# The last two attention steps of a fused linear-attention and routed-expert kernel: slots before attention rows, routing and plan before queries, unpaced scatters, first loads that wait for less

## The chip, the core and the metric

The kernel runs on one core of a Trainium2 chip. The metric is the device time of one launch in microseconds (us). A core has five engines with a queue each, which meet only at semaphores: PE (TensorE, matmuls), DVE (VectorE), ACT (ScalarE), POOL (GpSimd) and SP (SyncE, which here only issues DMAs).

## The reference

Input `x` is 16 batches of 512 tokens of width 256. The output is `x` plus a linear attention of the normalised rows plus a mixture of experts of the same rows.

```python
xn = layernorm(x)
Q, K, V = elu(xn @ Wq.T + bq) + 1, elu(xn @ Wk.T + bk) + 1, xn @ Wv.T + bv
attn = (Q @ (K.T @ V)) / (Q . (K.sum over tokens + 1e-6)) @ Wo.T + bo
scores = sigmoid(xn @ gate.T)           # 16 experts in 4 groups
# the best 2 groups by their two best scores, then the best 4 experts,
# weights = scores / their sum * 2.5
moe = sum over the 4 experts of weight * (silu(xn @ up[e]) @ down[e])
shared = silu(xn @ shared_up) @ shared_down
out = x + attn + moe + shared
```

## The kernel before, in words

There are two phases. In the **first phase** a loop over `c` = 0 to 15 (`B` = 16) takes one batch of 512 tokens a step: normalise, turn on PE, keys, queries, the product of keys and rows (`m`), its product with the folded output weights (`p`), the attention rows (`c_done`, `attention_rows`), and the shared expert in four parts (`up`, `down`, ending in `shared_sum`, which sets `y_summed`). Each fp32 product is made as three fp32r matmuls of a high and a low half (`split3`, L319); the halves are split by ACT (a cast) and DVE (a subtraction, the `..._low` and `..._split` functions).

Routing goes alongside, on DVE: `route_scores` to `route_experts` choose four experts for each token, PE counts ranks (`rank_batch`), `route_slots` and `route_chain` turn the ranks into row numbers and set `route_ready`. POOL then writes each normalised row, with its weights, to its slot in a buffer in HBM sorted by expert (`rows_by_expert`): 16 indirect scatters of 128 rows a batch, 12 of half rows (`scatter_row`, L498) and 4 of whole rows (`scatter_first`, L504), the latter with the sum of `x`, attention and shared expert in the second half. In the loop each scatter waits for a point of PE's work (pacing); those of batch c run during step c + 1. The last step has no successor: batch 14 is scattered in it, and batch 15 after it.

After the last routing DVE makes the **plan** (`count_units`, `plan_units`, `plan_rows`): which 256 rows each of the 143 units (`UNITS`) takes, of which expert, and which scatters must have landed before. PE turns it (L1482, L1484), DVE writes it as `table` (L1252) and as packed expert numbers (`packed`, L1258, `plan_ready`), and the engines load both into registers.

In the **second phase** unit u takes 256 rows of one expert. SP loads the first halves of its rows (`load_rows`, L428, 7 units ahead) and the second halves (`load_sums`, L438, 4 ahead). PE turns the rows (`turn_rows`), does the up product, and the down product (`unit_down`, sets `fd_done`); ACT casts and applies silu; DVE weighs and adds (`sum_up`, L1291, sets `y_ready`); POOL scatters the sums onward to the token's next slot with two indirect DMAs of 128 half rows (L587, L590 for the last units). PE's order in iteration u is up(u), turn(u + 2), down(u - 1), so rows u + 2 that are late hold unit u - 1 as well. From unit 6 on POOL also waits until PE is a unit ahead (`fd_done` of u + 2). In iteration 12 SP first loads one expert's weights into the only raw buffer, which is free when DVE has made the halves of the one before (`set_low`, iteration 6).

Which loads wait for batch 15: `load_rows` of units below 8 (`EARLY`) for what the table says, `load_sums(4)` for all its scatters, because the buffers `f_y[4]` to `f_y[7]` lie where the rows of batch 15 are scattered from; `load_rows(4)` for its attention rows.

## Time and profile before

| | us |
|---|---|
| median of 3 runs | 843.58 (842.2 to 844.42) |
| the profiled execution's own time | 846.81 |
| its span, first to last instruction | 845.1 |
| first phase, to the end of batch 15's scatters on POOL | about 455 |
| second phase, from the first unit's scatter on POOL | 457.9 to 836 |

The page has, over the span, PE 88% busy, DVE 83%, POOL 69%, ACT 68%; the issue of a DMA is not counted as busy. The span is to be read in two parts, since the phases have different limits, and at the seam between them.

### The profile page before, as it was taken

How to read it: one execution, taken by the hardware profiler on the slowest of the kernel's cores; microseconds unless marked ns; L12 is line 12 of the kernel's file. 1: busy time of each engine (PE TensorE's matmuls, PEld its weight loads, DVE VectorE, ACT ScalarE, POOL GpSimd, SP SyncE). 2: the span in 40 equal slices, each digit the busy share in tenths (PEclk: the TensorE clock that was granted, in tenths of full speed). 3: DMA queues.
4: the chain of work that ended last, by engine and by line, in shares of the span. 5: the costliest groups of instructions: out<-in, count | busy, mean ns of one | idle time of the engine just before them, and what ended most of it. 6: DMA issues, size and time to landing. Idle time of an engine off the chain costs nothing.

```text
span 845.1 us, 19794 instructions
## 1 busy us (share of the span) xinstructions
PE 744.0 (88%) x5232; PEld 678.8 (80%) x5232; DVE 698.6 (83%) x2401; ACT 572.8 (68%) x1174; POOL 581.7 (69%) x581
## 2 busy tenths in 40 slices
PE   4999999999999999999968798888979897989671
PEld 3899999999999999999857787777778777878661
DVE  5989999999999999999996788778868787878661
ACT  4877778777778777787615687676757676767540
POOL 1056777777677777776776677777777777777753
PEclk9999999999999999999997999999999999999985
DMA  6245544556445544433338999999999999999988
GB/s 178 69 158 202 206 155 166 200 184 216 174 147 198 184 157 147 144 123 117 114 134 275 297 352 309 328 337 333 342 319 319 323 348 325 330 331 338 332 267 271
DMA packets 142317, 199.66 MB, mean 236 GB/s; under 512 B 16752, under 2 KB 117760, under 8 KB 142208
## 3 DMA queue, kind: packets, MB, share of 16 engines
q1 hardware_dynamic: 111152, 113.41, 43.0%
q0 software_dynamic: 28064, 81.93, 25.2%
q10 hardware_dynamic: 2992, 3.06, 1.2%
q8 instruction: 45, 0.74, 0.4%
q14 instruction: 64, 0.52, 0.2%
HBM read 104.19 MB, written 105.04 MB: 248 GB/s over the span
## 4 chain that ended last, share of the span: by engine, by line
PE 46%; DMA 17%; DVE 16%; issue 9%; POOL 6%; SPq 3%; ACT 1%; DVEq 1%; ACTq 0%; POOLq 0%
PE bank_a L319 21%; PE bank_x L319 10%; PE bank_y L319 9%; DMA xn<-rows_by_expert 8%; DMA rows_by_expert<-xn,f_id 7%; DVE xn L1291 3%; POOL rows_by_expert L587 3%; PE bank_a L1495 3%; DMA x_in<-rows_by_expert 3%; DVE hs_l L1304 2%; POOL rows_by_expert L498 2%; PE bank_a L1334 1%; SPq L326 1%; SPq L438 1%; DVE w L1270 1%
## 5 line engine op out<-in xcount | busy, mean ns | idle before, releaser
L587 POOL DMA_INDIRECT rows_by_expert<-xn,f_id x256 | 249.8, 976 | 85.6 <-issue 50.6
L498 POOL DMA_INDIRECT rows_by_expert<-xn,slots_now x192 | 197.2, 1027 | 103.1 <-issue 44.3
L721 ACT CAST xt_h<-bank_a 128x512 fp32r<-128x512 f32 x143 | 84.0, 587 | 68.2 <-PE bank_a L1495 63.2
L1273 DVE TENSOR_TENSOR xt_l<-bank_a,xt_h 128x512 fp32r<-128x512 f32 x143 | 98.1, 686 | 23.9 <-ACT xt_h L721 23.4
L319 PE MATMUL bank_y<-ws,hs_h 128*128 128x256 f32 x512 | 96.4, 286 | 0.5 <-DVE hs_l L1029 0.5
L504 POOL DMA_INDIRECT rows_by_expert<-xn,slots_now x64 | 80.7, 1260 | 17.9 <-issue 14.2
L319 PE MATMUL bank_x<-xt_h,ws 128*128 128x512 f32 x256 | 92.0, 400 | 0.1
L752 ACT ACTIVATE hid<-bank_x 128x256 f32<-128x256 f32 x143 | 55.0, 384 | 53.9 <-PE bank_x L319 44.7
L319 PEld LDWEIGHTS bank_y<-ws,hs_h 128*128 128x128 f32 x512 | 82.6, 192 | 4.0 <-DVE hs_l L1029 0.7
L319 PE MATMUL bank_y<-ws,hs_l 128*128 128x256 f32 x256 | 73.2, 286 | 0.0
L319 PE MATMUL bank_y<-we,hs_h 128*128 x284 | 63.5, 316 | 10.9 <-DVE hs_l L1304 7.1
L319 PE MATMUL bank_a<-we,hs_h 128*128 x288 | 64.0, 315 | 9.5 <-DVE hs_l L1304 5.7
L669 ACT ACTIVATE k_f<-bank_a,minus_one 128x256 f32<-128x256 f32 x64 | 30.4, 476 | 54.7 <-issue 27.0
L1495 PE MATMUL bank_a<-ident,xn 128*128 128x128 f32 x288 | 47.9, 291 | 21.7 <-DMA xn<-rows_by_expert 21.2
L319 PE MATMUL bank_x<-xt_h,k_h 128*128 128x256 f32 x288 | 65.6, 290 | 0.1
L319 PE MATMUL bank_x<-xt_h,k_l_p 128*128 128x256 f32 x284 | 64.5, 289 | 0.4 <-DVE xt_l L1273 0.4
L1291 DVE SCALAR_TENSOR_TENSOR xn<-bank_a,w,xn 128x256 f32<-128x256 f32 x144 | 62.6, 475 | 0.8 <-PE bank_a L319 0.8
L1495 PE MATMUL bank_a<-ident,x_in 128*128 128x128 f32 x284 | 45.5, 283 | 19.9 <-DMA x_in<-rows_by_expert 19.1
L319 PEld LDWEIGHTS bank_y<-we,hs_h 128*128 128x128 f32 x284 | 46.1, 196 | 20.2 <-issue 18.7
L1291 DVE SCALAR_TENSOR_TENSOR xn<-bank_y,w,xn 128x256 f32<-128x256 f32 x142 | 61.7, 475 | 0.0
L1304 DVE TENSOR_TENSOR hs_l<-hid,hs_h 128x256 fp32r<-128x256 f32 x143 | 59.6, 417 | 2.5 <-ACT hs_h L757 2.5
L319 PEld LDWEIGHTS bank_a<-we,hs_h 128*128 128x128 f32 x288 | 46.3, 194 | 18.3 <-issue 17.5
(287 smaller groups left out, 2429.6 us busy)
## 6 DMA issues: line engine op xcount, KB each, us to landing
xn<-rows_by_expert SPq DMA_DIRECT2D x204, 272.0 KB, 4.8
x_in<-rows_by_expert SPq DMA_DIRECT2D x71, 272.0 KB
rows_by_expert<-spare SPq DMA_DIRECT2D x22, 544.0 KB, 5.4
x_in<-in_L_attn_x_dram SPq DMA_DIRECT2D x16, 512.0 KB, 4.0
out_dram<-rows_by_expert SPq DMA_DIRECT2D x8, 1024.0 KB, 14.9
rows_by_expert<-xn,f_id POOLq DMA_INDIRECT x286
rows_by_expert<-xn,slots_now POOLq DMA_INDIRECT x256
xn<-rows_by_expert ACTq DMA_DIRECT2D x11, 272.0 KB, 6.6
```

The lines of the kernel that those rows point to most:

```text
L319: last = nc.tensor.matmul(dst, a, b, start=start and k == 0, stop=stop and k == n - 1, skip_group_check=mixed)
L326: fours[engine, i] = fours.get((engine, i), ())[-4:] + nc.values_load_multi_w_load_instructions(table[i:i + 1, u // P, u % P:u % P + 4], e ...
L498: G.indirect_dma_start(out=half_rows[:, :], in_=xn[:, c % NB, s, 0:RW], in_offset=None, out_offset=bass.IndirectOffsetOnAxis(ap=slots_now[ ...
L504: G.indirect_dma_start(out=by_expert[:, :], in_=xn[:, c % NB, s, :], in_offset=None, out_offset=bass.IndirectOffsetOnAxis(ap=slots_now[:, ...
L587: G.indirect_dma_start(out=half_rows[:, :], in_=f_y[u % YB][:, tile], in_offset=None, out_offset=offset).then_inc(added[u % CLS], 16)
L669: S_.activation(k_f[:, s, :], A[s][:, 0:D], ACT.Exp, bias=minus_one[:, 0:1])
L721: S_.copy(f_h[u % 4], A[u % 2][:, :].rearrange("p (c s t) -> p c s t", c=KD, s=2)).then_inc(fx_hi, 1)
L752: S_.activation(f_hid[u % 2], X[u % 2][:, 0:UR], ACT.Silu).then_inc(fs_done, 1)
L1273: V.tensor_tensor(f_l[u % 4], A[u % 2][:, :].rearrange("p (c s t) -> p c s t", c=KD, s=2), f_h[u % 4].bitcast(F32), ALU.subtract).then_inc ...
L1291: last = V.scalar_tensor_tensor(out=y, in0=f_dn[u % 2][tile][:, 0:D], scalar=w2[:, u % 4, tile:tile + 1], in1=y, op0=ALU.mult, op1=ALU.add)
L1304: V.tensor_tensor(f_hl[u % 2], f_hid[u % 2], f_hh[u % 2].bitcast(F32), ALU.subtract).then_inc(fh_lo, 1)
L1495: last = T_.transpose(A[u % 2][:, (2 * h + tile) * P:(2 * h + tile + 1) * P], f_rows[u % RB][:, tile, h * P:(h + 1) * P], ident[:, :])
```

## The change

Five groups of edits, all around the last two steps (c = 14 and c = 15) and the first units:

1. **Step 14**: PE counts the ranks before the attention rows and DVE does `route_slots` and `route_chain` before `attention_rows`. One shared `down` moves from behind the keys of step 15 to ahead of them. The keys of step 15 go to the banks in the order in which the attention rows free them (`key_bank`), the ranks to another bank (`rank_bank`).
2. **Step 15 and the plan**: on DVE the routing of batch 15 comes right after the keys, and the whole plan before the `queries`, the low halves of queries and products, and the attention rows. PE puts the ranks before `m`, and the attention rows behind the turned plan. The table and the packed numbers are signalled apart (`table_ready`), and SP waits only for the table. Each of PE, DVE and ACT loads one word of expert numbers (six units) at first and the other 23 in iteration 2.
3. **POOL**: the scatters of batches 13, 14 and 15 wait for `route_ready` and `y_summed` only, in the order 12 half-row scatters, 4 whole-row scatters. The wait for PE's lead starts at unit 10, not 6.
4. **SP's first loads**: `f_y[4]` to `f_y[7]` move to other memory. The sums of units 4 to 6 are loaded before the rows of unit 7 and no longer wait for batch 15's scatters; the rows of unit 8 do (as they did, by their place in the queue).
5. **Expert weights**: one more expert's weights are made in the second phase. Loads stand in SP's iterations 12 and 26 (12 alone before), the splitting in iterations 3 to 6, 16 to 20 and 30 to 34. In iteration 1 PE does `unit_down(0)` before `turn_rows(2)`.

```diff
--- before.py
+++ after.py
...
-        per_batch = reused(q_f, (2, B + 1, E))
-        table = reused(q_f, (2, P), 0, COLS).bitcast(U32)
...
+        per_batch = reused(k_f, (2, B + 1, E), E * E + 8 * E)
+        table = reused(k_f, (2, P), 0, COLS).bitcast(U32)
...
-        f_y = [reused(xn, (2, RW), (i + 4) % 8 * 2 * RW) for i in range(YB)]
+        f_y = [reused(xn, (2, RW), (i + 4) * 2 * RW) for i in range(4)]
+        f_y += [reused(k_f, (2, RW), SUB * D - 2 * RW), reused(q_f, (2, RW)), reused(spare, (2, RW)),
+                reused(x_in, (2, RW), 4 * 2 * RW)]
...
-        LAST_SET_LOADED = 12
+        SET_LOADED = {12: SH + E - 2, 26: SH + E - 1}
+        SET_SHAPED = {3: SH + E - 3, 16: SH + E - 2, 30: SH + E - 1}
+        SET_HIGH = {4: SH + E - 3, 18: SH + E - 2, 32: SH + E - 1}
+        SET_LOW = {6: SH + E - 3, 20: SH + E - 2, 34: SH + E - 1}
...
+        def key_bank(c, s):
+            return A[(s + 2) % SUB if c == B - 1 else s]
+
+        def rank_bank(c):
+            return X[0 if c >= B - 2 else 1]
...
-                load_set(c + 3)
+                if c + 1 < B:
+                    load_set(c + 3)
...
-            sp.wait_ge(plan_ready, 1)
+            sp.wait_ge(table_ready, 1)
...
+                if u == EARLY:
+                    sp.wait_ge(scattered[(B - 1) % NB], scatters_until(B - 1))
                 sp.dma_start(f_rows[u % RB], unit_rows(row, 0)).then_inc(rows_loaded[u % RB], 16)
 
             def load_sums(u):
-                if u == 4:
-                    sp.wait_ge(scattered[(B - 1) % NB], scatters_until(B - 1))
+                if u == 5:
+                    sp.wait_ge(q_lo, B)
                 if u >= YB:
                     sp.wait_ge(added[(u - YB) % CLS], adds_until(u - YB))
                 for k in range(CLS):
...
+                if u in SET_LOADED:
+                    load_set(SET_LOADED[u])
+                if u == EARLY - 1:
+                    for v in range(EARLY // 2, EARLY - 1):
+                        load_sums(v)
                 if u < UNITS:
                     load_rows(u)
-                if 0 <= u - (ROWS_AHEAD - SUMS_AHEAD) < SUMS_BY_ACT:
-                    load_sums(u - (ROWS_AHEAD - SUMS_AHEAD))
+                v = u - (ROWS_AHEAD - SUMS_AHEAD)
+                if 0 <= v < EARLY // 2 or EARLY - 1 <= v < SUMS_BY_ACT:
+                    load_sums(v)
...
-            for c in range(B):
+            for c in range(B - 2):
...
+            ROWS = SUB * (TOP_K - 1)
+            scatter_row(B - 4, 10)
+            scatter_row(B - 4, 11)
+            pool.wait_ge(attn_ready, SUB * (B - 2))
...
+            for c in range(B - 3, B):
+                pool.wait_ge(route_ready, c + 1)
+                for n in range(ROWS):
+                    if c == B - 3 and n == 7:
+                        inverse_root(B - 1)
+                    scatter_row(c, n)
+                pool.wait_ge(y_summed, c + 1)
+                for s in range(SUB):
+                    scatter_first(c, s)
 
...
-                    if u >= 6:
+                    if u >= 10:
...
+            def queries_high(c):
+                act.wait_ge(q_ready, KD * (c + 1))
+                wait(act, c_done, SUB * c)
+                S_.copy(q_h[:, :, :], q_f[:, :, :]).then_inc(q_hi, 1)
...
+            queries_high(B - 1)
...
-                if c >= 1:
+                if 1 <= c < B - 1:
                     route_chain(c - 1)
                 for s in range(SUB):
                     dve.wait_ge(k_exp, SUB * c + s + 1)
...
                 route_scores()
+                if not after:
+                    route_inverse(c)
+                    route_group_scores()
+                    route_groups()
+                    route_top()
+                    route_experts()
+                    rows_split(c)
+                    dve.wait_ge(k_hi, c + 1)
+                    dve.wait_ge(c_done, SUB * c)
+                    V.tensor_tensor(k_l[:, :, :], k_f[:, :, :], k_h[:, :, :].bitcast(F32), ALU.subtract
+                                    ).then_inc(k_lo, 1)
+                    route_slots(c)
+                    shared_sum(c - 1)
+                    route_weights(c)
+                    route_chain(c)
+                    dve.wait_ge(m_hi, c + 1)
+                    V.tensor_tensor(m_l[:, :, :], A[2][:, :].rearrange("p (c d) -> p c d", c=KD),
+                                    m_h[:, :, :].bitcast(F32), ALU.subtract).then_inc(m_lo, 1)
+                    hidden_low(n)
+                    hidden_low(n + 1)
+                    count_units()
+                    plan_units()
+                    break
...
+                if c == B - 2:
+                    route_slots(c)
+                    route_chain(c)
+                    attention_rows(c)
+                    hidden_low(n + 3)
+                    continue
...
+            queries(B - 1)
             hidden_low(SH * B - 2)
-            hidden_low(SH * B - 1)
             dve.wait_ge(plan_turned, 1)
+            V.tensor_copy(table, X[0][0:COLS, 0:UR].rearrange("p (j u) -> p j u", j=2)).then_inc(table_ready, 1)
+            products_low(B - 1)
+            dve.wait_ge(plan_turned, 2)
...
             V.tensor_copy(packed, packed_f).then_inc(plan_ready, 1)
+            queries_split(B - 1)
+            hidden_low(SH * B - 1)
             attention_rows(B - 1)
             dve.wait_ge(attn_ready, SUB * B)
             shared_sum(B - 1)
 
             dve.wait_ge(plan_ready, 1)
-            experts = load_experts(mybir.EngineType.DVE)
+            experts = load_experts(mybir.EngineType.DVE, slice(0, 1))
...
                 for s in range(SUB):
-                    if s < 2:
+                    if not after:
+                        pe.wait_ge(attn_ready, SUB * (c - 1) + s + 1)
+                    elif s < 2:
                         wait(pe, attn_ready, SUB * (c - 1) + s + 3)
...
+                elif after:
                     down(n - 2)
                 for h in range(KD):
-                    pe.wait_ge(k_ready, SUB * c + h + 1)
+                    pe.wait_ge(k_ready, SUB * c + h + (1 if after else 3))
...
+                if not after:
+                    pe.wait_ge(silu_done, n + 1)
+                    rank_batch(c, rank_bank(c))
...
-                else:
-                    pe.wait_ge(q_ready, KD * (c + 1))
-                    rank_batch(c, A[0])
...
-                if after:
-                    up(n + 3, par)
+                if not after:
+                    break
+                up(n + 3, par)
+                if c == B - 2:
+                    pe.wait_ge(silu_done, n + 3)
+                    rank_batch(c, rank_bank(c))
                 pe.wait_ge(p_lo, KD * (c + 1))
                 pe.wait_ge(q_lo, c + 1)
                 for s in range(SUB):
-                    if s >= 2 and after:
+                    if s >= 2:
                         pe.wait_ge(xt_lo, KD * (c + 1) + s - 1)
-                    if s == 2 and not after:
-                        pe.wait_ge(rank_read, c + 1)
+                    attend(c, s)
+                if c == B - 2:
+                    down(n + 2)
+                    pe.wait_ge(rank_read, c + 1)
+                else:
                     pe.wait_ge(silu_done, n + SH)
-                    rank_batch(c, X[1])
-                if after:
-                    up(n + SH, (c + 1) % 2)
-                else:
-                    for i in range(2):
-                        down(n + i)
-                        up(n + 2 + i, par)
-
+                    rank_batch(c, rank_bank(c))
+                up(n + SH, (c + 1) % 2)
+
+            down(SH * B - 4)
+            down(SH * B - 3)
+            pe.wait_ge(rank_read, B)
+            up(SH * B - 2, (B - 1) % 2)
+            up(SH * B - 1, (B - 1) % 2)
             pe.wait_ge(plan_made, 1)
             pe.wait_ge(silu_done, SH * B)
...
+                last.then_inc(plan_turned, 1)
             down(SH * B - 2)
+            pe.wait_ge(p_lo, KD * B)
+            pe.wait_ge(q_lo, B)
+            for s in range(SUB):
+                attend(B - 1, s)
             down(SH * B - 1)
...
                 if u == 1:
+                    unit_down(0)
                     turn_rows(2)
-                    unit_down(0)
+                    unit_down(1)
                     turn_rows(3)
-                    unit_down(1)
...
```

Where instructions stand now and then, first on DVE from the end of the plan (the writes of `u_tab`) to the shared sum of batch 15. Before:

```order
L1167 TENSOR_SCALAR u_tab<-u_class_n 128x4x2
L1029 TENSOR_TENSOR hs_l<-hid,hs_h 128x512 x2
L1252 CAST q_f<-bank_x 7x256
L1253 TENSOR_TENSOR q_f<-bank_x,place 1x144
L1256 TENSOR_REDUCE q_f<-q_f 1x24
L1258 CAST q_f<-q_f 1x24
L1058 RECIPROCAL rz<-bank_a 128x2
L1061 SCALAR_TENSOR_TENSOR xn<-bank_a,rz,x_in 128x256 x2
L1058 RECIPROCAL rz<-bank_a 128x2
L1061 SCALAR_TENSOR_TENSOR xn<-bank_a,rz,x_in 128x256 x2
L1045 TENSOR_TENSOR xn<-bank_y,xn 128x4x256
```

After (L1067 queries, L1056 hidden low half, L1293 table, L1084 products' low halves, L1296 to L1301 packed numbers, L1072 queries' low half, L1091 first of the attention rows):

```order
L1200 TENSOR_SCALAR u_tab<-u_class_n 128x4x2
L1067 SCALAR_TENSOR_TENSOR q_f<-q_f,bank_a 128x512 x2
L1056 TENSOR_TENSOR hs_l<-hid,hs_h 128x512
L1293 CAST k_f<-bank_x 7x256
L1084 TENSOR_TENSOR k_l_p<-bank_a,k_l_p 128x258 x2
L1296 TENSOR_TENSOR k_f<-bank_x,place 1x144
L1299 TENSOR_REDUCE k_f<-k_f 1x24
L1301 CAST k_f<-k_f 1x24
L1072 TENSOR_TENSOR q_l<-q_f,q_h 128x1024
L1056 TENSOR_TENSOR hs_l<-hid,hs_h 128x512
L1091 RECIPROCAL rz<-bank_a 128x2
```

The queries' two instructions and the low halves of queries and products now stand behind the plan; they stood before it.

On POOL, towards the end of the first phase. Before (`x12` counts DMAs in a row; the first row is the last 6 half-row scatters of batch 13 and the first 6 of batch 14, the 18 are the last 6 of batch 14 and the 12 of batch 15):

```order
L498 DMA rows_by_expert<-xn,slots_now 237568x272 x12
L534 MEMSET x_in 128x256
L536 AFFINE_SELECT x_in<-x_in 128x256
L504 DMA rows_by_expert<-xn,slots_now 118784x544 x4
L498 DMA rows_by_expert<-xn,slots_now 237568x272 x18
L504 DMA rows_by_expert<-xn,slots_now 118784x544 x4
```

After, from the first half row of batch 13 on:

```order
L520 DMA rows_by_expert<-xn,slots_now 237568x272 x7
L516 TENSOR_TENSOR rstd<-var_eps,minus_half 128x4
L520 DMA rows_by_expert<-xn,slots_now 237568x272 x5
L526 DMA rows_by_expert<-xn,slots_now 118784x544 x4
L520 DMA rows_by_expert<-xn,slots_now 237568x272 x12
L526 DMA rows_by_expert<-xn,slots_now 118784x544 x4
L520 DMA rows_by_expert<-xn,slots_now 237568x272 x12
L526 DMA rows_by_expert<-xn,slots_now 118784x544 x4
```

Each batch is now a block of 12 and 4; the reciprocal root of step 15 (`rstd`) stands inside the block of batch 13, and batch 14's whole rows stand behind its half rows.

## Rows read from the trace of the kernel before

**Rows 1.** The page: busy time, share of the span, instructions, by engine.

```profile
PE 744.0 (88%) x5232; PEld 678.8 (80%) x5232; DVE 698.6 (83%) x2401; ACT 572.8 (68%) x1174; POOL 581.7 (69%) x581
```

**Rows 2.** Stretches: length, busy (x instructions) PE, PEld, DVE, ACT, POOL, clock, DMA share, GB/s.

```profile
450.00:460.00 10.00, 9.11 (x50) 8.61 (x51) 5.70 (x17) 4.96 (x11) 6.00 (x7) 0.66 0.99 337
...
600.00:700.00 100.00, 85.97 (x633) 76.43 (x631) 78.57 (x236) 70.90 (x159) 75.92 (x79) 0.98 0.98 328
```

**Rows 3.** Timeline of POOL: start, us, instruction [idle before, releaser].

```profile
411.94 0.96 POOL L498 DMA_INDIRECT rows_by_expert<-xn,slots_now  x1 [1.33 <-DVE xn L1024]
...
454.46 0.96 POOL L504 DMA_INDIRECT rows_by_expert<-xn,slots_now  x1 [0.30 <-issue]
...
457.90 0.96 POOL L587 DMA_INDIRECT rows_by_expert<-xn,f_id  x1 [2.47 <-DVE xn L1291]
...
486.42 0.96 POOL L587 DMA_INDIRECT rows_by_expert<-xn,f_id  x1 [0.30 <-DVE f_id L1286]
...
798.84 0.98 POOL L590 DMA_INDIRECT rows_by_expert<-xn,f_id  x1 [0.30 <-DVE f_id L1286]
```

**Rows 4.** Waits from 500 to 800 us: total us, times, longest.

```profile
POOL rows_by_expert L587 <- issue: 45.8, 150, 0.3
```

**Rows 5.** Timeline of DVE in step 15, as above.

```profile
415.68 1.27 DVE L1196 SCALAR_TENSOR_TENSOR q_f<-q_f,bank_a 128x512 f32<-128x512 f32 x2
...
424.95 1.22 DVE L1039 TENSOR_TENSOR q_l<-q_f,q_h 128x1024 fp32r<-128x1024 f32 x1
...
426.08 0.75 DVE L1051 TENSOR_TENSOR k_l_p<-bank_a,k_l_p 128x258 fp32r<-128x258 f32 x2
...
440.45 0.17 DVE L1167 TENSOR_SCALAR u_tab<-u_class_n 128x8 f32<-128x8 uint32 x1
```

**Rows 6.** Timeline of DVE from the shared sum into the first units.

```profile
447.52 1.23 DVE L1045 TENSOR_TENSOR xn<-bank_y,xn 128x1024 f32<-128x1024 f32 x1 [1.61 <-PE bank_y L319]
...
450.03 0.30 DVE L1270 COPY w<-xn 128x2 f32 x1 [1.28 <-issue]
...
456.75 0.88 DVE L1291 SCALAR_TENSOR_TENSOR xn<-bank_a,w,xn 128x256 f32<-128x256 f32 x2 [0.78 <-PE bank_a L319]
...
472.85 0.87 DVE L1291 SCALAR_TENSOR_TENSOR xn<-bank_y,w,xn 128x256 f32<-128x256 f32 x2
...
484.00 0.86 DVE L1291 SCALAR_TENSOR_TENSOR xn<-bank_y,w,xn 128x256 f32<-128x256 f32 x2
...
488.62 0.87 DVE L1291 SCALAR_TENSOR_TENSOR xn<-bank_y,w,xn 128x256 f32<-128x256 f32 x2
```

**Rows 7.** Chain of work: start, us, what; a step's attention rows, then one shared down.

```profile
329.69 3.01 PE bank_a L319 x24
332.70 1.44 PE bank_y L319 x12
```

**Rows 8.** Timeline of PE at the seam.

```profile
440.68 0.59 PE L1482 MATMUL bank_x<-ident,u_tab 128*7 128x128 f32 x2 [5.01 <-DVE u_tab L1167]
...
448.38 0.63 PE L1495 MATMUL bank_a<-ident,xn 128*128 128x128 f32 x4 [0.96 <-DMA xn<-rows_by_expert]
450.40 1.12 PE L1495 MATMUL bank_a<-ident,xn 128*128 128x128 f32 x4 [1.40 <-DMA xn<-rows_by_expert]
...
470.24 0.94 PE L1495 MATMUL bank_a<-ident,xn 128*128 128x128 f32 x4 [2.39 <-DMA xn<-rows_by_expert]
```

**Rows 9.** Timeline of SP's queue in the first units.

```profile
445.31 2.29 SPq L428 DMA_DIRECT2D xn<-rows_by_expert  x4
...
462.23 0.37 SPq L428 DMA_DIRECT2D x_in<-rows_by_expert  x1
...
465.88 0.38 SPq L428 DMA_DIRECT2D xn<-rows_by_expert  x1
...
474.35 0.82 SPq L371 DMA_DIRECT2D w_raw<-in_L_ffn_expert_up_dram  x2
...
477.44 0.39 SPq L428 DMA_DIRECT2D x_in<-rows_by_expert  x1
```

More of the change, by code:

```diff
@@ L571, in _ @@
-            pool.wait_ge(y_summed, B)
-            for s in range(SUB):
-                scatter_first(B - 1, s)
+                    pool.wait_ge(down_done, SH * c + 1)
+                    scatter_first(last, 2)
+                    pool.wait_ge(up_done, SH * c + 3)
+                    scatter_first(last, 3)
+                    pool.wait_ge(down_done, SH * c + 2)
+                    scatter_row(last, 6)
+                    pool.wait_ge(xt_done, c + 2)
+                    scatter_row(last, 7)
@@ L691, in _ @@
                 hidden_high(n + 1)
-                act.wait_ge(q_ready, KD * (c + 1))
-                wait(act, c_done, SUB * c)
-                S_.copy(q_h[:, :, :], q_f[:, :, :]).then_inc(q_hi, 1)
+                if after:
+                    queries_high(c)
                 act.wait_ge(m_done, c + 1)
@@ L1035, in rows_split, with queries @@
                                 ).then_inc(xr_lo, 1)
+            def queries(c):
+                for h in range(KD):
+                    dve.wait_ge(q_exp, KD * c + h + 1)
+                    V.scalar_tensor_tensor(out=q_f[:, h], in0=q_f[:, h], scalar=1.0, in1=A[h][:, :],
+                                           op0=ALU.min, op1=ALU.max).then_inc(q_ready, 1)
             def queries_split(c):
@@ L1193, in _ @@
                     set_eps_rows()
-                for h in range(KD):
-                    dve.wait_ge(q_exp, KD * c + h + 1)
-                    V.scalar_tensor_tensor(out=q_f[:, h], in0=q_f[:, h], scalar=1.0, in1=A[h][:, :],
-                                           op0=ALU.min, op1=ALU.max).then_inc(q_ready, 1)
+                queries(c)
                 if c == 0:
@@ L1299, in _ @@
                     sum_up(1)
+                    experts += load_experts(mybir.EngineType.DVE, slice(1, WORDS))
                 if 1 < u and u + 2 < UNITS:
@@ L1397, in rank_batch, with attend @@
                 last.then_inc(rank_done, 1)
+            def attend(c, s):
+                cols = slice(s * P, (s + 1) * P)
+                split3(A[(s + 2) % SUB][:, 0:PW],
+                       [(q_h[:, d, cols], q_l[:, d, cols], p_h[:, d, :], p_l[:, d, :])
+                        for d in range(KD)]).then_inc(c_done, 1)
             for c in range(B):
@@ L1486, in _ @@
-            last.then_inc(plan_turned, 1)
+            for bank, columns in ((X[0][0:COLS, :], slice(0, COLS)), (X[1][0:1, :], slice(1, 2))):
+                for j in range(2):
+                    last = T_.matmul(bank[:, j * P:(j + 1) * P], u_tab[:, j, columns], ident[:, :],
+                                     start=(j == 0), stop=True, skip_group_check=True)
+                last.then_inc(plan_turned, 1)
             down(SH * B - 2)
+            pe.wait_ge(p_lo, KD * B)
+            pe.wait_ge(q_lo, B)
```

159 lines of the change are left out of this document (57 added, 102 removed).

## The prediction

> **What bounds the kernel now.** I read the page first, and it misleads. PE is busiest with 88%, POOL stands at 69% [rows 1], but the issue of an indirect DMA holds POOL longer than its row shows: between two scatters of the second phase it stands 0.30 us in "issue", whatever else is ready [rows 4]. From the stretches, 600 to 700 us has 79 instructions on POOL, 75.92 us busy [rows 2]; 79 x (0.96 + 0.30) = 99.5 of 100 us. So POOL is full there. Its timeline says from when: unit 9's first scatter starts at 486.42, unit 131's at 798.84, 122 units in 312.42 us = 2.56 a unit, against 2 x 1.26 = 2.52 with no gap at all [rows 3]. PE's 0.86 and DVE's 0.79 of that stretch are slack. The DMA share of 0.98 [rows 2] does not free the scatters' own pace, and I take it as the runner-up.
>
> So the end stands a fixed distance behind the time at which POOL comes to its full pace, about unit 9 or 10. Before, POOL's last scatter of batch 15 starts at 454.46, unit 0 at 457.90 after 2.47 us idle, and the nine units to 486.42 take 28.52, where 9 x 2.54 = 22.9 would do (2.54 lies between the 2.52 and the 2.56 above): 5.7 us lost [rows 3]. What sets unit 9 is y. DVE adds y of unit 5 at 472.85, unit 9 at 484.00, unit 11 at 488.62: 2.31 a unit at the end, faster than POOL [rows 6]. Ahead of unit 5 PE waits 2.39 us for the rows of unit 8 [rows 8], which SP issues at 465.88, after those of unit 7 at 462.23 [rows 9]; unit 7's wait for the last scatter of batch 15 to land (7.8 us from 454.46, issue to landing). That chain starts with the last whole rows of batch 15, which need the shared sum, at 448.75 [rows 6]. After DVE's plan ends (440.45 + 0.17 = 440.62, rows 5) PE has waited 5.01 us [rows 8].
>
> **The change, part by part.**
>
> *The plan first (2).* Out of DVE's way to the plan come the two queries (one row of 1.27 for both), the low half of q 1.22 and the low halves of the products 0.75 [rows 5]: 1.27 + 1.22 + 0.75 = 3.2, of which I count 3.0, since parts are passed in the shadow of waits. Against it, a down of 1.44 [rows 7] now stands ahead of step 15's keys; half of it is in the shadow of DVE and ACT, so 0.75 against. The plan ends 440.62 - 3.0 + 0.75 = 438.4, 2.2 earlier. The routing work that comes into step 14 lies beside PE's work, at 0; if that cover were gone it would cost some of the two routing chains' DVE time, which I bound by 1 us.
>
> *What now stands behind the plan (2).* Queries 1.2, a hidden half 0.6, the table 0.4, products 0.7, packed numbers 0.75 (small instructions of 0.2 each), the low half of q 1.15: q is ready at 438.4 + 4.8 = 443.2. Only then PE does the attention rows, 24 matmuls in 3.01, and the last down 1.44 [rows 7]: 447.65 at full clock. The stretch 450 to 460 has a granted clock of 0.66 against 0.98 later [rows 2], and behind the 5.01 us wait at 440.68 the transposes are slow (0.59 for two, and 1.12 for four at 450.40 where the same four took 0.63 at 448.38, rows 8). So between 4.45 (all at the upper level, 2.4 GHz) and 8.9 us (all at 1.2 GHz); I take 5.4, since the PE wait before it is shorter now: 448.6. The shared sum of 1.23 [rows 6] then ends at about 450.0 (449.1 to 453.3), against 448.75. Here the change loses 1.3 us.
>
> *Scatters (3).* The 28 scatters of batches 14 and 15 that need no sum of batch 15 take, from 411.94, 28 x 1.26 = 35.3: 447.2 [rows 3]; the sum is later than that, so POOL waits for the sum alone and the last four start by 450.0 + 0.2 + 3 x 1.26 = 454.0, against 454.46. The change gains 0.5 here. Before, the last one could have started at 448.75 + 0.2 + 3.8 = 452.7 by the sum; POOL was 1.7 us behind it with half rows. Those 1.7 us, now gone, pay for the sum that comes 1.3 later. The Trainium skill ("DMA: Bandwidth & Descriptors", section on the anatomy of a GpSimd DMA) gives such a transfer 2.0 us plus its bytes at 436 GB/s. By the page a whole-row scatter of 128 x 2,176 bytes would be 2.6 us, where this trace shows 7.8 with the last four and earlier ones in the queues; by it the rows would be there some 3 us sooner, an estimate, and by the page the sum would change by under 1 us, since PE's own pace then binds.
>
> *SP's loads (4).* The rows 0 to 3 were issued at 445.31 [rows 9], some 4.7 behind the plan. SP no longer waits for the packed numbers, and the plan is 2.2 earlier: 442, so PE finds the rows of units 0 to 3 there and drops its waits of 0.96 and 1.40 [rows 8]. Before, y of unit 0 starts at 448.75 + 8.0 = 456.75 [rows 6]; now at 450.0 + 8.0 - 2.36 = 455.6. The first six units' numbers cost fewer register words now: 1.28 us for 24 words before the first unit [rows 6] become 0.3, and the other 23 come in iteration 2, between 0 (DVE idles there as long) and 1.2 us; I take 0.2. From y 0 to y 5 is 16.1 us now, of which 2.39 is PE's wait for unit 8's rows. If that is gone, y 5 stands at 455.6 + 13.7 + 0.2 = 469.5.
>
> Is it gone? The last scatter now lands 7.8 us after its start, with a DMA share of 0.99 [rows 2]; the lower bound is a row load, 465.88 to 470.24 = 4.4 [rows 8, 9]. I take 7.0, somewhat less load at its side: 461.0. The rows of unit 7 go there, those of 8 one us later (sums 4 to 6 now stand in front, so SP's distance of 3.65 [rows 9] shrinks to that): 462.0, landed 466.4, y 5 2.61 later [rows 6, 8] = 469.0. The two ways meet; the later, 469.5, holds: **3.3 us before** 472.85. Unit 12's rows (477.44 now, rows 9), unit 9's y and POOL follow it by as much. Without the 2.39 wait PE's slow clock behind it, at 470 to 475, falls away as well: another 0.5, estimated as half a unit's PE time of which half is hidden. **Sum: 3.8 us.**
>
> *Unpaced units (3).* POOL in units 6 to 9 waits for PE no longer, but in them it waits for y anyway; 0. It can put its scatters closer to SP's loads, and takes DMA share from them: up to 1 us against.
>
> *One more set in the second phase (5).* It holds SP's queue for about 3 us in iteration 26, as it does in iteration 12 (474.35 to the rows at 477.44, rows 9), and costs ACT and DVE some instructions, by the kinds in rows 5 and 6 at most 1.2 each. DVE and PE have 14 to 21% to spare against POOL by then [rows 2]; 0. If the cover were gone: 3 us, which is all of the gain.
>
> **Numbers.** The profiled execution takes 846.81, the median is 843.58; 3.2 apart. 846.81 - 3.8 = 843.0 profiled, 843.58 - 3.8 = **839.8** in the median.
>
> **Rivals.**
>
> - *A larger gain.* The landing takes 4.4 us, the registers nothing, PE's clock stays at the upper level (sum ready at 449.1), step 14's slots earlier give PE a free start into step 15. Then y 5 stands at 467 or before, and POOL's start is bound by its own scatters: 5.7 + 2.2 idle us of the seam can go at most, less 1. 843.58 - 6.6 = 837. For it: POOL's idle time is there; against: y of unit 0 isn't earlier than the sum allows. 0.17.
> - *No change.* The time at which POOL fills doesn't matter as much as I think, since the DMA queues at 0.98 [rows 2] set the pace from 490 on and take back what POOL gains; or the second set's loads at iteration 26 run dry the rows once. 843.58 - 0.5 = 843. For it: the DMA share; against: POOL's 2.56 a unit against its own minimum of 2.52, on 122 units. 0.22. The Trainium skill ("Perfetto Trace Analysis", What "DMA-bound" means) names two limits that fit here, the 16 DMA engines themselves or the sequencer that issues, told by its solid track; by the first the result is this rival's 843, by the second the forecast, and this trace has both signs, 0.98 of DMA share and a POOL without gaps.
> - *Slower.* One mechanism: the attention rows and the last down behind the turned plan run at 1.2 GHz (the 5.01 wait and the slow rows behind it speak for it), the shared sum ends at 453.3, the last scatter starts at 457.3 and lands at 465, unit 8's rows go at 466, and y 5 stands at 473.1 or behind 453.3 + 5.6 + 13.9 = 472.8, with the clock's loss continuing in units 0 to 2 (some 2 us). It breaks even at a sum at 452.8 and is slower by 0.3% (2.5 us, about what a measurement can tell from no change) from 455.4 on. Against: PE is less idle than before, as it does up and attention in the gap. 845.2 to 847. 0.11.
>
> **How the numbers follow.** The forecast, 838 to 841.2, has 0.50; larger 0.17, no change 0.22, slower 0.11. The range takes in the landing and the clock on both sides: 835 to 844.5, with under 0.2 left out. Faster by over 0.3% is below 841.1: 0.50 + 0.17 = 0.67; 0.22; 0.11.
>
> **What would show it.** The plan's last write at 438.4, q's low half at 443.2 and the shared sum at 450 (a step is wrong by what each differs). POOL's first whole row of batch 15 waits for DVE's sum, and its last starts at 454.0. SP's rows of 0 to 3 at 442, unit 8's at 462 with no PE wait of over 1 us for them. y 5 at 469.5; POOL's unit 9 at about 482.6; then 2.56 a unit, and unit 131 at 795.0. A pace other than 2.56, a stall of POOL behind iteration 26, or a sum behind 452.8 would make it wrong.

## The result, and the profile after

The changed kernel takes 849.85 us in the median of 7 runs (847.81 to 851.62), the kernel before 844.42 in 7 runs beside it: a ratio of 1.0056, 95% interval 1.004 to 1.0072. It is slower, and outside the range of the prediction. Its profiled execution took 849.55 us with a span of 847.7. Two single executions further on, one of e7 and one of the kernel before beside e17 and e18, took about 1771 us and are left out of every ratio.

The busy line of its page answers to [rows 1] and tells as little as that one did:

```profile
PE 739.0 (87%) x5232; PEld 673.5 (79%) x5232; DVE 698.0 (82%) x2401; ACT 572.0 (67%) x1174; POOL 580.3 (68%) x581
```

The stretches (columns as in [rows 2]), with one more, 460 to 470:

```profile
450.00:460.00 10.00, 6.31 (x50) 5.64 (x49) 7.06 (x18) 5.83 (x12) 5.65 (x6) 1.00 0.90 282
460.00:470.00 10.00, 4.28 (x22) 4.08 (x23) 2.01 (x7) 2.69 (x7) 2.10 (x3) 0.66 0.98 338
600.00:700.00 100.00, 84.98 (x629) 75.96 (x628) 78.14 (x236) 70.41 (x158) 75.91 (x80) 0.98 0.99 330
```

In 600 to 700 nothing moved. In 460 to 470 every compute engine is idle for more than half of the time, POOL 7.9 of 10 us, with the DMA queues full. The timeline of POOL, which answers to [rows 3], has the place:

```profile
452.78 0.96 POOL L526 DMA_INDIRECT rows_by_expert<-xn,slots_now  x1 [3.57 <-DVE xn L1078]
...
456.66 0.96 POOL L526 DMA_INDIRECT rows_by_expert<-xn,slots_now  x1 [0.30 <-issue]
457.96 0.96 POOL L603 DMA_INDIRECT rows_by_expert<-xn,f_id  x1 [0.34 <-DVE xn L1336]
...
472.05 0.96 POOL L603 DMA_INDIRECT rows_by_expert<-xn,f_id  x1 [9.01 <-DVE xn L1336]
...
493.91 0.96 POOL L603 DMA_INDIRECT rows_by_expert<-xn,f_id  x1 [1.52 <-PE bank_y L324]
```

The first row is batch 15's first whole-row scatter: POOL waits 3.57 us for the shared sum, as forecast. Unit 0 follows the last one at once. Then, ahead of unit 2 at 472.05, POOL stands 9.01 us, which was forecast nowhere. Unit 10 starts at 493.91 against 488.95 before. DVE and PE in the same stretch (timeline, the answers to [rows 5, 6, 8]):

```profile
416.73 0.19 DVE L917 TENSOR_SCALAR r_den<-r_exp 128x64 f32<-128x64 f32 x1
...
441.69 0.17 DVE L1200 TENSOR_SCALAR u_tab<-u_class_n 128x8 f32<-128x8 uint32 x1
...
451.28 1.23 DVE L1078 TENSOR_TENSOR xn<-bank_y,xn 128x1024 f32<-128x1024 f32 x1 [0.41 <-PE bank_y L324]
...
459.68 0.87 DVE L1336 SCALAR_TENSOR_TENSOR xn<-bank_y,w,xn 128x256 f32<-128x256 f32 x2
466.60 0.17 DVE L1315 COPY w<-x_in 128x2 f32 x1 [6.06 <-issue]
```

```profile
457.75 0.60 PE L1554 MATMUL bank_a<-ident,xn 128*128 128x128 f32 x4
465.18 0.55 PE L324 MATMUL bank_x<-xt_h,k_l_p 128*128 128x256 f32 x1 [6.84 <-issue]
...
466.60 1.06 PE L1554 MATMUL bank_a<-ident,x_in 128*128 128x128 f32 x4
```

"Issue" is time in which the engine waited for nothing that the profile shows. Both pauses stand exactly where the program loads the 23 remaining words of expert numbers into registers (iteration 2), and such a load has no row of its own. PE's pause costs a little more than its length: behind it the granted clock is 0.66 in 460 to 470, and four transposes at 466.60 take 1.06 us where the same four took 0.60 at 457.75. Two rows of SP (answer to [rows 9]) say when the first rows were issued, and when the rows of unit 7 went, 6.3 us behind the last scatter:

```profile
445.18 2.29 SPq L446 DMA_DIRECT2D xn<-rows_by_expert  x4
...
462.93 0.37 SPq L446 DMA_DIRECT2D x_in<-rows_by_expert  x1
```

### The profile page after: what moved, and what is told of

The parts are those of the page before. It is cut to its first block, busy times and chain, and to the rows that moved or that the text cites. A ratio compares the mean times of both kernels' runs of the same rounds, so it can differ in the third digit from the quotient of the medians.

```text
span 847.7 us, 19798 instructions
## 1 busy us (share of the span) xinstructions
PE 739.0 (87%) x5232; PEld 673.5 (79%) x5232; DVE 698.0 (82%) x2401; ACT 572.0 (67%) x1174; POOL 580.3 (68%) x581
## 3 DMA queue, kind: packets, MB, share of 16 engines
q0 software_dynamic: 28064, 81.93, 25.1%
## 4 chain that ended last, share of the span: by engine, by line
PE 46%; DMA 20%; DVE 14%; issue 8%; POOL 6%; SPq 3%; ACT 1%; DVEq 1%; ACTq 1%; POOLq 0%
PE bank_a L324 22%; PE bank_x L324 10%; PE bank_y L324 9%; DMA rows_by_expert<-xn,f_id 6%; DMA x_in<-rows_by_expert 6%; POOL rows_by_expert L603 3%; DMA xn<-rows_by_expert 3%; PE bank_a L1554 2%; POOL rows_by_expert L520 2%; DMA rows_by_expert<-spare,f_id 1%; DVE hs_l L1350 1%; PE bank_a L1380 1%; SPq L334 1%; SPq L456 1%; DMA rows_by_expert<-q_f,f_id 1%
## 5 line engine op out<-in xcount | busy, mean ns | idle before, releaser
L603 POOL DMA_INDIRECT rows_by_expert<-xn,f_id x128 | 124.5, 972 | 49.4 <-issue 25.0
L324 PE MATMUL bank_y<-we,hs_h 128*128 x284 | 61.3, 308 | 9.5 <-DVE hs_l L1350 5.1
L324 PE MATMUL bank_x<-xt_h,k_h 128*128 128x256 f32 x288 | 63.5, 283 | 1.2 <-DVE xt_l L1318 1.2
L1554 PE MATMUL bank_a<-ident,xn 128*128 128x128 f32 x288 | 45.8, 283 | 16.6 <-DMA xn<-rows_by_expert 16.2
L324 PEld LDWEIGHTS bank_y<-we,hs_h 128*128 128x128 f32 x284 | 44.2, 188 | 19.6 <-issue 18.5
L784 ACT CAST hs_h<-hid 128x256 fp32r<-128x256 f32 x143 | 58.6, 409 | 0.1
L324 PEld LDWEIGHTS bank_x<-xt_h,k_l_p 128*128 128x128 f32 x284 | 49.9, 194 | 7.0 <-issue 7.0
```

Of the source, the lines that this page charges most:

```text
L324: last = nc.tensor.matmul(dst, a, b, start=start and k == 0, stop=stop and k == n - 1, skip_group_check=mixed)
L603: G.indirect_dma_start(out=half_rows[:, :], in_=f_y[u % YB][:, tile], in_offset=None, out_offset=offset).then_inc(added[u % CLS], 16)
L784: S_.copy(f_hh[u % 2], f_hid[u % 2]).then_inc(fh_hi, 1)
L1554: last = T_.transpose(A[u % 2][:, (2 * h + tile) * P:(2 * h + tile + 1) * P], f_rows[u % RB][:, tile, h * P:(h + 1) * P], ident[:, :])
```

## The experiments

"e5", "e7" and so on are short for the runs whose names begin so. Each ratio is to executions of the kernel before on the same chip. e1 to e4 and e13 to e16 ran on two slower chips, on which the kernel before takes 966 and 973 us: in e1 the stretch 600 to 700 has a DMA share of 0.84 at 259 GB/s, a granted clock of 0.91 and 61 POOL instructions where [rows 2] has 0.98, 328, 0.98 and 79. From these runs only pauses inside a trace are read closely. The others ran on three chips on which it takes 843 to 844 us, called the faster chips.

### Are the words the loss? (e1, e2, e5, e6)

e1 and e5 are the changed kernel with all words ahead of unit 0, in PE, DVE and ACT alike; e2 and e6 are the kernel before with the change's late load.

```diff
 # e1, e5: changed kernel
-            experts = load_experts(mybir.EngineType.DVE, slice(0, 1))
+            experts = load_experts(mybir.EngineType.DVE, slice(0, WORDS))
...
-                    experts += load_experts(mybir.EngineType.DVE, slice(1, WORDS))
 # e2, e6: kernel before
-            experts = load_experts(mybir.EngineType.DVE)
+            experts = load_experts(mybir.EngineType.DVE, slice(0, 1))
...
                 if u == 2:
                     sum_up(1)
+                    experts += load_experts(mybir.EngineType.DVE, slice(1, WORDS))
```

> The changed kernel, but PE, DVE and ACT each load all 24 words of expert numbers before unit 0, and none in iteration 2. Theory 1 (the late load is the loss): the 9.0 us in which POOL stands before unit 2 fall to under 3, since the 6 to 7 us of issue time that PE, DVE and ACT show in iteration 2 go; the words cost 1.3 us before unit 0 as in the kernel before; POOL's unit 10 starts near 489 instead of 493.9, and the time falls by 3 to 5 us, to 845 to 847. Rival 2 (unit 2 is late through its rows or DMAs anyway): the gap at unit 2 stays over 6 us under another name and the time stays at 849 to 850. Rival 3 (the load costs 6 us wherever it stands once DMAs are busy): a gap of 6 us moves ahead of unit 0, same time as the changed kernel.

> The kernel before, with one word of expert numbers loaded before unit 0 and 23 in iteration 2, as the change does. Theory 1: PE, DVE and ACT stand 6 to 7 us in iteration 2, POOL's unit 10 moves from 488.95 to about 493, the time rises by 2 to 5 us to 846 to 848. Rival 2 (the delay belongs to the new order of rows and sums, not to the words): nothing of it here, 843 to 844.5.

Measured: e1 1.0143 (1.0113 to 1.0174) and e2 1.0033 (1.0014 to 1.0051), on a slower chip. There the changed order has further stalls that neither kernel shows on the faster chips (ACT stands 21.7 us in step 15 of e1), so the expectations could not be settled by e1's time; e2's trace already had PE's pause of 6.8 us. Once more:

> The kernel of e1_words_at_once once more (24 words of expert numbers before unit 0, none later), for a chip on which the kernel before takes 844 us and not 966. Theory 1: POOL's idle time before unit 2 falls from 9.0 us to under 3, its unit 10 starts at 489 or before, the time is 844 to 847. Rivals as there: 849 to 850.

> The kernel of e2_before_split_words once more (the kernel before, with 23 of its 24 words loaded in iteration 2). There PE showed 6.8 us and DVE 5.8 us of issue time in iteration 2, as in the changed kernel. Theory 1: the same pause here, POOL's unit 10 at 492 to 494, and 2 to 5 us above the kernel before: 846 to 849. If the time stays at 844, the pause is covered and the words don't explain the loss.

Measured: e5 843.5 us, ratio 0.9999 (0.9983 to 1.0014): the whole loss is gone. e6 847.98 us, 1.0044 (1.0028 to 1.0059): the late words alone make the kernel before slower by nearly as much. In e5 POOL's unit 10 starts at 487.17. Behind batch 15's last scatter its timeline of POOL has no long wait left; the longest is the first row, ahead of unit 0, and the other is unit 10:

```profile
459.27 0.96 POOL L603 DMA_INDIRECT rows_by_expert<-xn,f_id  x1 [2.10 <-DVE xn L1334]
...
487.17 1.02 POOL L603 DMA_INDIRECT rows_by_expert<-xn,f_id  x1 [1.08 <-PE bank_y L324]
```

In e6's timelines PE and DVE stand in iteration 2 as in the changed kernel:

```profile
465.96 0.55 PE L319 MATMUL bank_x<-xt_h,k_l_p 128*128 128x256 f32 x1 [8.80 <-issue]
```

```profile
466.91 0.17 DVE L1272 COPY w<-x_in 128x2 f32 x1 [7.01 <-issue]
```

There POOL stands 10.73 us ahead of unit 2, as it stood 9.01 in the changed kernel. Theory 1 holds, rivals 2 and 3 fall.

### Number, place or form of the load? (e3, e9, e10, e13, e14, e15)

Why were 24 words cheap ahead of unit 0 (1.28 us, rows 6) and 23 dear in iteration 2? These are all the changed kernel with another split of the words, the same in PE, DVE and ACT.

```diff
 # e3: 1 word before unit 0, 5 in iteration 2, 18 in iteration 20
+                    experts += load_experts(engine, slice(1, 6))
+                if u == 20:
+                    experts += load_experts(engine, slice(6, WORDS))
 # e9: both loads before unit 0
             experts = load_experts(engine, slice(0, 1))
+            experts += load_experts(engine, slice(1, WORDS))
 # e10: 1 word before unit 0, all 24 in iteration 2
+                    experts = load_experts(engine, slice(0, WORDS))
 # e13: 8 before, 16 late; e14: 4 before, 20 late, slice(4, WORDS)
+                    experts += load_experts(engine, slice(8, WORDS))
 # e15: 1 before, the first 23 in iteration 2, the last in iteration 60
+                    experts = load_experts(engine, slice(0, WORDS - 1))
```

> The changed kernel, with 5 of the 23 words loaded in iteration 2 and 18 in iteration 20. If each word has its price (6.1 to 6.8 us for 23, 0.27 to 0.3 each), the pause in iteration 2 is 1.4 us and one of 5 us stands in iteration 20, where DVE's and PE's lead over POOL hides most of it: time 846 to 848. If the load has a fixed price whatever its length, both pauses are 6 us and the time is 849 to 852. If it is the traffic in iteration 2, the pause in iteration 20 tells by its size per word.

> The changed kernel, with its two loads of 1 and 23 words both before unit 0. If the price of the 23 words comes from the form of the load (a part of the row of words that starts at its second one, or a second load), a pause of 6 to 7 us now stands ahead of unit 0 and the time stays at 848 to 850. If it comes from the place in iteration 2 (rows, sums and scatters in flight), the pause is under 1.5 us and the time is that of e5, 843 to 845.

> The changed kernel, but the load of iteration 2 takes all 24 words from the first on, in one piece, as the kernel before does before unit 0. If the place sets the price: PE, DVE and ACT stand 6 to 7 us as in the changed kernel, time 848 to 851. If the form does: under 1.5 us, time 843 to 845.

> The changed kernel with 8 words before unit 0 and 16 words, from byte 32 of the row on, in iteration 2. If any start that is not the row's own is slow: 16 x 0.27 = 4.3 us of issue time on PE and DVE in iteration 2. If a boundary of 32 bytes or a count that is a multiple of 8 is enough: under 1.5 us.

> The changed kernel with 4 words before unit 0 and 20 words, from byte 16 on, in iteration 2. If 16 bytes are no sufficient boundary, 20 x 0.27 = 5.4 us of issue time in iteration 2; if they are, under 1.5 us. Slow here and quick in e13 sets the boundary between 16 and 32 bytes, or the count at a multiple of 8.

> The changed kernel with 23 words from the first on in iteration 2, and the last word alone in iteration 60. If the number of words sets the price, 6 to 7 us of issue time in iteration 2 as in the changed kernel. If the start does, under 1.5 us.

Measured: e9 851.24 us, 1.009 (1.007 to 1.0109), slower still and above the expected 848 to 850; the pause now stands ahead of unit 0, whose scatter starts at 466.11, and that nothing there covers it is a reading, not shown. e10 842.65 us, 0.9996 (0.9977 to 1.0015), as good as e5, and POOL stands 2.88 us ahead of unit 2. So the place is not the cause. e3 984.56 us, 1.0184 (1.0162 to 1.0206), e13 990.12, e14 991.27 and e15 988.55 us (the last three of one execution each) are from the slower chips; their DVE rows are what counts. First e9, DVE's first row of unit 0:

```profile
459.25 0.17 DVE L1315 COPY w<-xn 128x2 f32 x1 [8.14 <-issue]
```

e3, behind its 18 words in iteration 20:

```profile
562.69 0.17 DVE L1317 COPY w<-x_in 128x2 f32 x1 [3.57 <-issue]
```

and the row behind the load of iteration 2 in e10, e13, e14 and e15, in this order:

```profile
459.82 0.22 DVE L1315 COPY w<-x_in 128x2 f32 x1 [1.52 <-issue]
```

```profile
505.26 0.17 DVE L1315 COPY w<-x_in 128x2 f32 x1 [0.22 <-DVE xn L1336]
```

```profile
505.62 0.17 DVE L1315 COPY w<-x_in 128x2 f32 x1 [0.47 <-DVE xn L1336]
```

```profile
503.26 0.17 DVE L1317 COPY w<-x_in 128x2 f32 x1 [1.16 <-issue]
```

| load | begins at byte | DVE's pause, us |
|---|---|---|
| 23 words (changed kernel; e6; e9) | 4 | 6.06; 7.01; 8.14 |
| 18 words (e3) | 24 | 3.57 |
| 5 words (e3) | 4 | 0.31 |
| 24 words late (e10; e17; e18, which come below) | 0 | 1.52; 2.08; 2.27 |
| 24 words ahead of unit 0 (kernel before; e5; e7; e12) | 0 | 1.28; 0.91; 1.09; 0.94 |
| 23 words (e15) | 0 | 1.16 |
| 20 words (e14) | 16 | 0.47 |
| 16 words (e13) | 32 | 0.22 |

The number of words doesn't decide it (23 are dear from byte 4 and cheap from byte 0), nor does being a second load (e13, e14). What decides is where in the row of words a long load begins: 4 and 24 bytes are dear, 0, 16 and 32 cheap. A dear word costs 6.06 / 23 = 0.26 us (up to 8.14 / 23 = 0.35 in e9), a cheap one between 0.91 / 24 = 0.04 and 2.27 / 24 = 0.09. That 16 bytes is the boundary is read from these starts alone, each of 16, 24 and 32 from one execution on a slower chip; whether 8 would do wasn't tried. The load of iteration 2 stands behind two rows of `sum_up(1)` (0.87 us), and whether a part of it passes beneath them isn't known; so the pauses under 1 us, the 5 words of e3 among them, don't give a price by the word.

### The rest of the change (e4, e7, e8, e11, e12)

With the words out of the way, the other parts were undone one at a time. e4 and e7 put back the order of step 14 and the start of step 15; e8 puts back SP's first loads; e11 moves e7's words into waits; e12 puts e7's second set back into step 14.

```diff
 # e4, e7: on e5
 def key_bank(c, s):
-    return A[(s + 2) % SUB if c == B - 1 else s]
+    return A[s]
...
-                if c == B - 2:
-                    route_slots(c)
-                    route_chain(c)
-                    attention_rows(c)
-                    hidden_low(n + 3)
-                    continue
 # e8: on e5
-                if u == 5:
-                    sp.wait_ge(q_lo, B)
+                if u == 4:
+                    sp.wait_ge(scattered[(B - 1) % NB], scatters_until(B - 1))
 # e12: on e7
-        SET_LOADED = {12: SH + E - 2, 26: SH + E - 1}
+        SET_LOADED = {12: SH + E - 1}
```

> The kernel of e1_words_at_once with step 14 and the start of step 15 in the order of the kernel before: ranks and slots of batch 14 behind its attention rows, one down behind the keys of step 15, keys in banks 0 to 3. Theory 1: the keys of step 15 end near 413 instead of 416.8, the plan 2 to 3.5 us earlier (438.5 to 440), the shared sum near 449.5 instead of 452.5, and the time is 1 to 3 us below that of e1. Rival: the routing of batch 14 then stands in front of step 15's keys again and eats what is won, so the plan ends within 0.7 us of e1's and the time is the same.

> The kernel of e4_step14_as_before once more: e5 with step 14 and the start of step 15 in the order of the kernel before. Theory 2 (the order of step 14 costs the keys 3.9 us and the plan 3): the plan ends at 438 to 440, the shared sum at 449 to 450.5, time 1 to 3 us below e5. Rival: same as e5 within 1 us.

> The kernel of e5 with SP's first loads and the places of the sums as in the kernel before (rows of unit 7, then sums of unit 4 behind the last scatter of batch 15, then rows of unit 8). If the forecast was right that the new order of loads takes 2 to 4 us off, this is 2 to 3 us above e5 and PE waits some 2 us for the rows of unit 8. Rival: the scatters of batch 15 set the rows of units 7 and 8 in both, so it is within 1 us of e5.

> The kernel of e7, with PE's and DVE's 24 words loaded where both wait (PE ahead of the attention rows of batch 15, in its wait for the low half of the queries; DVE ahead of its attention rows, in its wait for PE) in place of behind them. DVE's 1.1 us of issue time before unit 0 and its idle 1.25 us fall together: unit 0's first scatter up to 1 us earlier, time 0 to 1 us below e7 (841.7 to 842.7 where the kernel before takes 843.6). Rival: the words take longer while the half rows of batch 15 are being written and delay the attention rows, 0.5 to 3 us above e7.

> The kernel of e7, with one set of expert weights in the second phase as in the kernel before and the other made in step 14. Forecast of the prediction: the second set costs nothing in the second phase, so the time is e7's plus what step 14 loses by the set (0 to 1.5 us; the plan ends that much later). Rival 1 (the second set holds back POOL by up to 3 us about unit 26 or its DMAs cost as much): 1 to 3 us below e7, and no POOL wait over 0.6 us between units 20 and 30.

| run | median us | ratio, 95% interval | plan ends | POOL's unit 10 |
|---|---|---|---|---|
| e4 (slower chips) | 980.23 | 1.0134, 1.0114 to 1.0154 | | |
| e5 | 843.5 | 0.9999, 0.9983 to 1.0014 | 441.1 | 487.17 |
| e7 | 842.74 | 0.9981, 0.9968 to 0.9995 | 438.3 | 484.98 |
| e8 | 844.44 | 1.0012, 0.9997 to 1.0027 | 439.9 | 487.51 |
| e11 | 843.6 | 1.0001, 0.9986 to 1.0015 | 438.6 | 487.24 |
| e12 | 842.51 | 0.999, 0.9977 to 1.0003 | 441.0 | 489.19 |

e7 is the only run that is faster than the kernel before beyond its interval, by 0.19% or 1.6 us, and one such interval among so many runs is weak evidence. Against e5 it gains 0.18% or 1.5 us by the ratios and 0.8 us by the medians, with intervals that overlap: the expected 1 to 3 us is not shown in the time, and e4 against e1, the same pair on a slower chip, shows nothing (1.0134 and 1.0143). The traces do show it in the plan. The row behind the four keys is at 413.2 to 413.5 in e7, e11 and e17, which have the old order of step 14, and at 414.5 to 416.7 in the five with the new one (the changed kernel, e5, e8, e9, e10); the plan ends 25.1 us later in all eight. On the mean the new order has both 2.1 us later. (All eight have the set out of step 14; with the old order and the set in it, the kernel before, e6, e12 and e18 have the keys at 412.9 to 415.9.) e8 loses 0.13% to e5 (1.1 us, the intervals overlap; 2 to 3 was forecast), and in its timeline PE waits for the rows of unit 8:

```profile
469.96 0.66 PE L1544 MATMUL bank_a<-ident,xn 128*128 128x128 f32 x4 [2.79 <-DMA xn<-rows_by_expert]
```

which e5 doesn't. e11 was a miss: unit 0's first scatter is at 455.94 against e7's 455.61, no earlier, and the time is 0.9 us above e7, as its rival had it. e12 is within 0.1% of e7, but its plan ends 2.7 us later, which could hide a gain. The profiled executions speak against that: from POOL's unit 10 to the end of the time e12 takes 355.9 us and e7, with the second set, 355.9 too, so the second set costs the second phase nothing that can be seen.

### A better version? (e16, e17, e18)

e16 and e17 are e7 with one word before unit 0 and all 24 in one piece in iteration 2; e18 is that on e12.

```diff
 # on e7 (e16, e17), on e12 (e18), in PE, DVE and ACT
-            experts = load_experts(engine, slice(0, WORDS))
+            experts = load_experts(engine, slice(0, 1))
...
+                if u == 2:
+                    experts = load_experts(engine, slice(0, WORDS))
```

> The kernel of e7 (step 14 and the start of step 15 as before) with one word before unit 0 and all 24 in one piece in iteration 2. The 1.1 us of issue time before unit 0 go and up to 1.5 us come in iteration 2, where e10 shows 1.5 on DVE; unit 0's scatter is 1 us earlier and unit 10's within 1 us of e7. Time 840.5 to 843 where the kernel before takes 843.5. Rival: the later shared sum and the landing of batch 15 hold unit 8's rows in both, and it is within 0.5 us of e7's ratio of 0.998.

> The kernel of e16 once more, for a chip on which the kernel before takes 844 us. POOL's unit 0 about 1 us earlier than in e7, unit 10 within 1 us of e7's 485.0. If the end follows unit 10, the ratio is 0.995 to 0.998; if a later wait (the landing of batch 15, then PE's rows of unit 8 and 11) takes the place of the one removed, it is e7's 0.998 again.

> The kernel of e17, with the second set of expert weights made in step 14 as in the kernel before. If the second set costs nothing in the second phase, it is 0 to 0.2% above e17 (step 14's work delays the plan by up to 1.5 us). If the set takes the forecast gain, it is 0.1 to 0.4% below e17.

Measured: e16 981.44 us, 1.01 (1.0072 to 1.0127), on a slower chip. e17 842.36 us, 0.9991 (0.9976 to 1.0005), unit 10 at 485.11; e18 844.15 us, 0.9996 (0.998 to 1.0012). e17's unit 0 comes 0.8 us before e7's (454.81 against 455.61), but units 1 to 3 give it back: POOL waits 3.55 us at 463.11. e18 is 0.05% above e17 by the ratios and 0.2% by the medians, inside the expected 0 to 0.2%. Neither beats e7, and no set of edits tried gave more than e7's 1.6 us.

## Why the prediction was wrong

**The step that failed** is in the part on SP's loads: "The first six units' numbers cost fewer register words now ... and the other 23 come in iteration 2, between 0 (DVE idles there as long) and 1.2 us; I take 0.2". It was 6.06 us on DVE and 6.84 on PE. I priced the load by its number of words, from a row on 24 words from byte 0, and took that as the upper bound for 23 from byte 4. The bound held for another form. The pause is worth 0.0056 + 0.0001 = 0.57% or 4.8 us (changed kernel to e5), the size and sign of the result. The Trainium skill ("Runtime: NRT & Kernel Launch", section "Instruction fetch mechanics") gives some 200 ns a register for its register loads (it speaks of words in HBM, here they lie in SBUF); an estimate by it is 4.6 us for 23 words. The dear form is above that (6.06), and the 24 words from byte 0 are far below it (0.04 to 0.09 us each); the runs decide. A price of this size would have been a rival in the prediction, and it was left out.

**Second, a term mis-sized:** "half of it is in the shadow of DVE and ACT, so 0.75 against" for the keys of step 15. DVE's row behind the four keys is at 412.90 before and at 416.73 after, but these are two extremes: it stands at 415.11 in e6, which has the first phase of the kernel before, and at 414.5 to 416.0 in the other four with the new order. Against the old order, with the set out of step 14 in both, the mean is 2.1 us later, and of that at most 1.5 us are seen in the time (e5 to e7, not clear of noise). Against the old order with the set in step 14 (the kernel before, e6, e12, e18) it is 0.8 us later: the set's leaving step 14, which the prediction gave no worth there, paid for most of it. It hardly is the down alone: the attention rows of step 14 stand behind the routing chain of batch 14 on DVE (411.61 for its last row, 411.91 for the first attention rows), and PE's keys wait for those rows' banks (0.89 us at 412.54). "at 0; if that cover were gone it would cost ... 1 us" was too little, if the down cost its 0.75; no run undid one of the two without the other.

**Third, a base.** The sum was made against an execution 3.2 us above the median, and its stalls at the seam were taken for those of every run. Across the twelve profiled executions on the faster chips, the time goes with POOL's unit 10: at 485.0 to 485.2 (e7, e10, e17) 840.9 to 843.0 us, at 493.9 to 495.8 (the changed kernel, e6, e9) 849.6 to 851.9. The pace from there on is the same (unit 130 less unit 10: 307.3 before, 306.6 after), so the end does follow unit 10. But in the kernel before it stood at 488.95 in an execution of 846.81. Executions with a time like its median have it near 487.2 (e5 844.17, e11 843.38), so in a median one it is some 1.8 us earlier, and e12, with 489.19, took 845.04: the rest of the 3.2 us lies behind unit 10. How much of e7's 4.0 us is this, a single profile can't show; the 1.6 us of the ratio fit with it. Taken without the base the forecast of the seam is good: e10, the changed kernel but for its load, has unit 9 at 481.84 (forecast 482.6) in an execution of 843.0 (forecast 843.0), and yet its ratio is 0.9996. The 3.8 us were gained on an execution, not on the kernel. What stretched that one execution stays open.

What the unpaced scatters (edit 3) do by themselves was not tried. Two sums of the prediction are off without touching its forecast: 5.7 + 2.2 - 1 is 6.9 and not 6.6, and a landing of 2.6 in place of 7.0 us is 4.4 sooner, not some 3.

**What held.** From the end of the keys to the end of the plan 27.7 us became 25.1: 2.6 saved, 3.0 forecast. POOL waits for the sum alone, and its last scatter starts 4.1 us behind it (forecast 4.0). The rows of unit 7, which wait for it to land, go 6.3 us behind its start (forecast 7.0). The rows of unit 8 hold nobody (edit 4, worth 0.13% in e8, not clear of noise; 3.3 us forecast with the rest of the seam). The steady pace and the second set: nothing, as said. PE's clock did not fall in 440 to 460 (granted 1.00 in both halves; [rows 2] had 0.66 for 450 to 460), so the rival "slower" did not come by its mechanism: the sum ended at 452.5, from the late keys (3.8 in this execution) and not from a slow PE. **What did not hold besides:** the first rows at 442 (445.18), since the table stands behind the queries and a hidden half on DVE (its row starts at 443.56), which the SP term forgot.

The rival "no change" has the size of e5, the changed kernel without its dear words, but not by its own reasons: the second set took nothing back, and the pace behind unit 10 stayed. The late keys and a base that was too slow account for most of it; how much each is not separated.

## What to carry to other kernels

A load of words into registers has no row in the profile: look for "issue" time on every engine that loads, and price it from a load of the same form, not only of the same length. If part of a table of words is loaded early and the rest late, let each part begin where the cheap ones here did (0, 16 or 32 bytes), or load the whole again. Before a gain is summed up from stalls, see whether other executions of the same kernel have them too: here most of the 3.8 us stood in one profile only. And before work is moved ahead of something that frees a buffer, look up who waits for that buffer: with the chain of batch 14 ahead of the attention rows, and one more product, the keys came 2.1 us later.

## What the runs showed of the hardware

A load of 23 register words from byte 4 of a row stops PE and DVE for 5.7 to 8.8 us, one of 23 or 24 words from byte 0 for 0.9 to 2.5 (0.91 on DVE in e5, 2.50 on PE in e18). And the same kernel took 843 to 844 us on three chips and 966 and 973 on two others. In e1, on one of these, the second phase moved 259 GB/s in place of 328, at a granted clock of 0.91 in place of 0.98, and a unit took 3.3 us in place of 2.56; an edit's ratio did not carry over (e7's 0.9981, and 1.0134 for the same kernel as e4).
